# The last head of a four-layer gated transformer: gated outputs and normalising moved from VectorE to ScalarE and GpSimd

## The reference

```python
x = x + jnp.tanh(g_xattn[3]) * _L3_xattn_ref(_layernorm(x, axis=-1), ctx_4096, ctx_4096, pos_BxS2, mask_BxSxS2_ik0, L3_xattn_Wq, L3_xattn_Wk, L3_xattn_Wv, L3_xattn_Wo)
x = x + jnp.tanh(g_ffn[3]) * _L3_ffn_ref(_layernorm(x, axis=-1), L3_ffn_A, L3_ffn_B, L3_ffn_Wr)
```

## Time and profile before

| | before |
|---|---|
| median of 3 runs | 2186.48 us (2184.53 to 2188.93) |
| the profiled execution | 2186.74 us |
| its span | 2184.9 us |
| mean granted TensorE clock | 0.912 of full speed |
| last turn, first to last tile's `add_out` | 2003.22 to 2162.09 us in the span |

### The profile page before, as it was taken

How to read it: one execution, slowest core, us unless ns; L and a number is a source line. 1 busy time by engine, 2 the same in 40 slices (tenths; PEclk the granted TensorE clock), 3 DMA queues, 4 the chain that set the end, 5 groups by cost and what they waited for, 6 DMA issues and landing times. The chain is left out here.

```text
span 2184.9 us, 37129 instructions
## 1 busy us (share of the span) xinstructions
PE 1860.1 (85%) x14832; PEld 1034.9 (47%) x14832; DVE 1671.9 (77%) x2989; ACT 557.4 (26%) x1290; POOL 599.5 (27%) x717
## 2 busy tenths in 40 slices
PE   4388788887788888988855899999999999999876
PEld 3344455444554355533632355555555555555432
DVE  3379766798658966699644788888888888888875
ACT  3121223222342123222224122222222222222221
POOL 0220114102140023300224443434343434343210
PEclk7689978999899987999967999999999999999987
DMA  7436501473033720436013211111111111110100
GB/s 231 154 103 191 152 2 39 132 204 111 1 103 115 204 63 1 137 116 174 1 43 127 78 49 49 49 49 49 49 50 51 52 51 51 49 30 20 40 25 35
DMA packets 134266, 176.47 MB, mean 81 GB/s; under 512 B 46416, under 2 KB 73200, under 8 KB 133968
## 3 DMA queue, kind: packets, MB, share of 16 engines
q1 hardware_dynamic: 134096, 174.10, 26.5%
HBM read 131.98 MB, written 42.08 MB: 80 GB/s over the span
## 5 line engine op out<-in xcount | busy, mean ns | idle before, releaser
L1156 POOL TENSOR_TENSOR early_vare<-early_mv,w_eps 128x1 f32<-128x1 f32 x96 | 30.1, 313 | 779.0 <-DVE early_mv L1222 764.9
L379 PE MATMUL la_ps<-w_xTh,w_wqh 128*128 128x512 bf16 x512 | 198.4, 388 | 15.4 <-DVE la_rot L2271 10.3
L2210 POOL TENSOR_TENSOR la_q<-la_straight,la_rot 128x512 f32<-128x512 f32 x128 | 163.1, 1274 | 164.7 <-DVE la_rot L2271 164.7
L379 PE MATMUL la_ps<-w_woh,la_oTh 128*128 128x512 bf16 x512 | 199.2, 389 | 0.0
L380 PE MATMUL la_ps<-w_wol,la_oTh 128*128 128x512 bf16 x512 | 198.8, 388 | 0.0
L750 PE MATMUL early_ps<-early_products,w_heads 128*32 128x512 f32 x1024 | 146.0, 698 | 61.0 <-DVE early_products L1373 34.9
L381 PE MATMUL la_ps<-w_woh,la_oTl 128*128 128x512 bf16 x512 | 197.8, 386 | 0.0
L380 PE MATMUL la_ps<-w_xTl,w_wqh 128*128 128x512 bf16 x512 | 196.7, 384 | 0.0
L381 PE MATMUL la_ps<-w_xTh,w_wql 128*128 128x512 bf16 x512 | 196.6, 384 | 0.0
L2223 POOL TENSOR_TENSOR la_p<-la_s,la_rec 128x256 f32<-128x256 f32 x128 | 89.6, 700 | 322.4 <-DVE la_rec L2292 322.4
L2161 ACT ACTIVATE la_oTh<-la_ps 128x256 bf16<-128x256 f32 x256 | 84.2, 381 | 303.1 <-PE la_ps L2073 303.1
(11 more groups left out here) (345 smaller groups left out, 4535.2 us busy)
## 6 DMA issues: line engine op xcount, KB each, us to landing
early_vR<-scr_v SPq DMA_DIRECT2D x128, 257.0 KB, 5.2
early_wkv<-wkv SPq DMA_DIRECT2D x32, 512.0 KB, 4.6
la_v<-v SPq DMA_DIRECT2D x64, 256.0 KB, 3.9
k<-early_ctxt SPq DMA_DIRECT2D x32, 256.0 KB, 3.7
v<-early_ctxt SPq DMA_DIRECT2D x64, 128.0 KB, 3.1
scr_p<-early_weights SPq DMA_DIRECT2D x16, 512.0 KB, 3.1
early_pR<-scr_p SPq DMA_DIRECT2D x32, 256.0 KB, 3.4
w_raw_q<-in_Wq SPq DMA_DIRECT2D x8, 1024.0 KB, 6.9
```

Of the source, the lines that this page charges most:

```text
L379: pe.matmul(out, lh[c], rh[c], start=(first and c == 0), stop=False)
L2210: rope_sum.send(pool.tensor_tensor(dst, straight[:, slot, :], rot[:, slot, :], ALU.add))
```

## The change

The last turn alone changes, in units 1 to 15 and behind them.

- **Output of the attention.** `add_out` of tiles 0 to 15 goes from VectorE. ScalarE copies the bank times the gate into `gated` (`out_copy`, two buffers in `raw_q`, free by then), and GpSimd adds it to x (`add_x`). `statistics` waits for `x_added`.
- **Normalising.** `normalised` goes from VectorE to ScalarE as one activation with scale and bias; GpSimd computes the bias (minus the mean times the factor) with two more small operations in `rstd_of`. ScalarE does `normalised(i-2)` behind `exponentials` and `route_exp` of unit i; VectorE did it at the end of unit i-1.
- **Output of the experts.** `final` goes from VectorE: ScalarE copies the bank times the gate into `moved` (`move_copy`), GpSimd adds x (`final`), and SyncE's stores wait for `finished` in place of the drained bank.
- **Low half of the turned x.** `low_x` goes from the gap behind the subtraction of the softmax to behind the rotation, before `statistics`.
- TensorE's stream is the same. One more constant is set (`minus_one`, with `pads` counted to 4).

The diff, cut to its core and shifted left by 8 columns:

```diff
+minus, offset, minus_one = sb("minus", [P, 2]), sb("offset", [P, 2]), sb("minus_one", [P, 1])
+gated, moved = raw_q[:, 0:2, :], raw_q[:, 2:4, :]
...
+x_added, offset_ready, finished = signal("x_added", UNITS), signal("offset_ready", UNITS), signal("finished", UNITS)
...
     for t in range(UNITS):
-        banks.wait_drained(sp, KV - 1, "add", t)
+        finished.wait(sp, 0, t)
         stored[t % 2].send(sp.dma_start(io["out"][t * P:(t + 1) * P, :], xout[:, t % 2, :]))
...
+    def out_copy(t):
...
+        banks.wait_filled(act, KV - 1, "out", t // QUAD, t % QUAD, "last")
+        banks.drain(act.activation(gated[:, t % 2, :], banks.bank("out", t // QUAD, t % QUAD, "last"), ACT.Copy,
+                                   scale=w["gates"][:, 3:4]), "out", t // QUAD, t % QUAD, "last")
+
+    def normalised(t):
+        offset_ready.wait(act, 0, t)
...
+        xn_ready.send(act.activation(xn[:, t % 2, :], w["X"][:, t, :], ACT.Identity,
+                                     scale=rstd[:, t % 2:t % 2 + 1], bias=offset[:, t % 2:t % 2 + 1]))
...
+    def move_copy(t):
...
+        banks.wait_filled(act, KV - 1, "add", t)
+        banks.drain(act.activation(moved[:, t % 2, :], banks.bank("add", t), ACT.Copy,
+                                   scale=w["gates"][:, 7:8]), "add", t)
...
                 if not more and i >= 3:
                     route_exp(i - 3)
                 if not more and i >= 2:
+                    normalised(i - 2)
                     high_x(i - 2)
                 banks.wait_filled(act, turn, "turn", n, u, *L)
                 banks.drain(act.activation(pT[:, u % 2, :, :].rearrange("p h k -> p (h k)"),
                                            banks.bank("turn", n, u, *L)[:, 0:2 * P], ACT.Copy),
                             "turn", n, u, *L)
+                if not more and i >= 1:
+                    out_copy(i - 1)
                 if not more and i >= 4:
...
                         oTh[:, u % 2, :, :].rearrange("p (a b) t -> p a b t", b=2)[:, :, half, :],
                         banks.bank(name, n, u, *L)[:, 0:2 * P].rearrange("p (h t) -> p h t", h=2), ACT.Copy))
+                if not more and i >= 4:
+                    move_copy(i - 4)
                 if not more and i >= 2:
                     route_copy(i - 2)
...
+                    normalised(i - 2)
                     high_x(i - 2)
+                if i == UNITS:
+                    out_copy(UNITS - 1)
                 hsT_copy(i - 4)
+                move_copy(i - 4)
                 if i - 2 < UNITS:
                     route_copy(i - 2)
...
     def rstd_of(t):
         s = slice(t % 2, t % 2 + 1)
...
         pool.tensor_tensor(vare[:, s], mv[:, t % 2, 1:2], w["eps"][:, :], ALU.add).then_inc(pool_step, 1)
+        pool.tensor_tensor(minus[:, s], mv[:, t % 2, 0:1], minus_one[:, :], ALU.mult).then_inc(minus_step, 1)
         pool.wait_ge(pool_step, t + 1)
+        if t >= 2:
+            xn_ready.wait(pool, 0, t - 2)
         rstd_ready.send(pool.tensor_tensor(rstd[:, s], vare[:, s], w["power"][:, 0:1], ALU.pow))
+        pool.wait_ge(minus_step, t + 1)
+        rstd_ready.wait(pool, 0, t)
+        offset_ready.send(pool.tensor_tensor(offset[:, s], minus[:, s], rstd[:, s], ALU.mult))
+
+    def add_x(t):
+        banks.wait_drained(pool, KV - 1, "out", t // QUAD, t % QUAD, "last")
+        x_added.send(pool.tensor_tensor(w["X"][:, t, :], w["X"][:, t, :], gated[:, t % 2, :], ALU.add))
+
+    def final(t):
+        banks.wait_drained(pool, KV - 1, "add", t)
+        if t >= 2:
+            stored[t % 2].wait(pool, 0, t // 2 - 1)
+        finished.send(pool.tensor_tensor(xout[:, t % 2, :], w["X"][:, t, :], moved[:, t % 2, :], ALU.add))
...
                 if more or (n, u) != (QUAD - 1, QUAD - 1):
                     divide(turn, QUAD * n + u + 1, (u + 1) % 2)
+                if not more and at >= 1:
+                    if at == 1:
+                        pool.wait_ge(pads, 4)
+                    add_x(at - 1)
+                if not more and at >= 5:
+                    final(at - 5)
                 for i, place, which, step in projections(n, u, more):
                     add_rotation(turn, place, (len(FIRST) + i) % 2, rotated(which, step))
...
                 if not more and (n, u) != (0, 0):
                     rstd_of(QUAD * n + u - 1)
         if not more:
+            add_x(UNITS - 1)
             rstd_of(UNITS - 1)
+            for t in range(UNITS - 5, UNITS):
+                final(t)
...
         shifted_ready.send(dve.tensor_tensor(s[:, slot, :, :], s[:, slot, :, :],
                                              mx[:, slot, :].unsqueeze(2).to_broadcast([P, GROUP, SEQ]),
                                              ALU.subtract))
-        if meanwhile is not None:
-            low_x(meanwhile)
         exp_ready.wait(dve, turn, i)
         st.link(dve.tensor_reduce(tot[:, slot, :], s[:, slot, :, :], AX.X, ALU.add))
         rec_ready.send(dve.reciprocal(rec[:, slot, :], tot[:, slot, :]))
...
     def statistics(t):
-        banks.wait_drained(dve, KV - 1, "out", t // QUAD, t % QUAD, "last")
+        x_added.wait(dve, 0, t)
         fs.link(dve.bn_stats(stats[:, t % 2, :], w["X"][:, t, :]))
         stats_ready.send(dve.bn_aggr(mv[:, t % 2, :], stats[:, t % 2, :]))
-
-    def normalised(t):
-        dve.wait_ge(rstd_ready.sem, t + 1)
-        xn_ready.send(dve.tensor_scalar(xn[:, t % 2, :], w["X"][:, t, :], mv[:, t % 2, 0:1],
-                                        rstd[:, t % 2:t % 2 + 1], ALU.subtract, ALU.mult))
...
-    def final(t):
-        banks.wait_filled(dve, KV - 1, "add", t)
-        if t >= 2:
-            stored[t % 2].wait(dve, 0, t // 2 - 1)
-        banks.drain(dve.scalar_tensor_tensor(out=xout[:, t % 2, :], in0=banks.bank("add", t),
-                                             scalar=w["gates"][:, 7:8], in1=w["X"][:, t, :], op0=ALU.mult,
-                                             op1=ALU.add), "add", t)
...
                 if prev:
                     lows(*prev)
-                if not more and i >= 5:
-                    final(i - 5)
                 if more or (n, u) != (QUAD - 1, QUAD - 1):
                     softmax(turn, st, ("score", n, u, *L), (u + 1) % 2, QUAD * n + u + 1,
-                            (QUAD * n + u + 1) % (QUAD * QUAD), i - 2 if not more and i >= 2 else None)
-                else:
-                    low_x(i - 2)
+                            (QUAD * n + u + 1) % (QUAD * QUAD))
                 for p, place, _, step in projections(n, u, more):
                     rotate(turn, len(FIRST) + p, (len(FIRST) + p) % 2, place, step)
-                if prev:
+                if prev and (more or i == 0):
                     add_out(*prev)
                 if (n, u) == (0, 0) and not is_first(turn):
                     banks.wait_drained(dve, turn - 1, "out", QUAD - 1, QUAD - 1)
                 if not more:
+                    if i >= 2:
+                        low_x(i - 2)
                     if i >= 1:
                         statistics(i - 1)
                     if i >= 3:
                         choose(i - 3)
-                    if i >= 1:
-                        normalised(i - 1)
         if more:
             st.close()
         else:
             lows(turn, QUAD - 1, QUAD - 1, *L)
-            for i in range(UNITS, UNITS + 5):
-                if i - 3 < UNITS:
-                    logits(i - 3)
-                final(i - 5)
+            for i in range(UNITS, UNITS + 3):
+                logits(i - 3)
                 if i - 2 < UNITS:
                     low_x(i - 2)
                 if i == UNITS:
-                    add_out(turn, QUAD - 1, QUAD - 1, *L)
                     statistics(UNITS - 1)
-                if i - 3 < UNITS:
-                    choose(i - 3)
-                if i == UNITS:
-                    normalised(UNITS - 1)
+                choose(i - 3)
```

More of the change, by code:

```diff
@@ L1862, in last_attention @@
         hs_ready = signal("hs_ready", UNITS)
+        x_added, offset_ready, finished = signal("x_added", UNITS), signal("offset_ready", UNITS), signal("finished", UNITS)
+        minus_step = new_semaphore(nc, w, "la_minus_step")
         stored = [signal(f"stored{p}", UNITS // 2, 16) for p in range(2)]
@@ L2134, in high_x @@
                                             ACT.Copy))
+            def out_copy(t):
+                if t >= 2:
+                    x_added.wait(act, 0, t - 2)
+                banks.wait_filled(act, KV - 1, "out", t // QUAD, t % QUAD, "last")
[4 more added lines that the diff above has]
+                if t >= 2:
+                    banks.wait_filled(act, KV - 1, "xturn", t - 2)
+                xn_ready.send(act.activation(xn[:, t % 2, :], w["X"][:, t, :], ACT.Identity,
+                                             scale=rstd[:, t % 2:t % 2 + 1], bias=offset[:, t % 2:t % 2 + 1]))
+            def move_copy(t):
+                if t >= 2:
+                    finished.wait(act, 0, t - 2)
```

(10 more changed lines are left out.)

## The result

The changed kernel takes 2231.31 us (median of 4 runs, 2218.19 to 2238.51) against 2187.7 for the kernel before (4 runs): a ratio of 1.0195, with a 95% interval of 1.016 to 1.0229. It is slower, as forecast, but by 43.6 us and not by 22, and it lies outside the range of 2199 to 2219. The profiled execution took 2227.45, 40.7 more than that of before.

What follows compares the result with a forecast made beforehand. The prediction took a loop through all of x's path as the bound. Second stretch 17.3, first 0.4, tail 2.4 and sharing 1.9 made 22.0 us more, 2208.5 us against the median of 2186.48, range 2199 to 2219.

Steps and rivals of the forecast that it cites:

- the faster rivals: Last turn, cases below the forecast: VectorE relief pays, 2175 (0.05); only first stretch gains, 2192 (0.05); nothing much, 2187 (0.03).
- Steps 1, 3 and 4: Loop after the output projection lands: copy and addition, statistics at 2.04 us; normalising starts at 6.86, takes 0.80.
- step 2: Loop, statistics and choice of experts on VectorE: stay at 2.21 us, ending 4.25 after the output projection lands.
- Step 3: Loop, ScalarE: normalising waits behind the next unit's exponentials, which wait for VectorE; starts 6.86 us after the landing.
- the first rival: Relief of VectorE pays, normalising not held behind exponentials: second-stretch period 10.4, first 14.3 us less, total 2175; chance 0.05.
- Step 5, second stretch: Last turn's later seven periods, turning of x to the next output projection's landing: 5.70 us, ends 5.16 and 6.5.
- The tail: From the last output projection's landing to the end of the last `final`: 18.84 us, 2.4 more than before.
- Step 5, first stretch: Last turn's first eight periods, turning of x to the next landing: 3.48 us, TensorE's idle time staying near 2.2.
- The sharing term: GpSimd's rotation sum slowing VectorE's choice in six first-stretch units: 0.31 us each, 1.9 in all, ends 0 and 7.6.
- the fallen clock: Rival: clock falls in the first stretch too, 3.48 becoming 5.16 in six units; 10 us more, 2218.5; chance 0.10.
- the full hold: Rival: GpSimd's additions hold VectorE up in full; 5.7 us more, 2214; chance 0.07.

Runs made afterwards that it cites:

- e2: The changed kernel with ScalarE's normalising put ahead of the exponentials; ratio 1.0025 to the kernel before.
- e1: The changed kernel with GpSimd's order alone altered, rotation sums ahead of `add_x` and `final` behind `rstd_of`; ratio 1.013 to the kernel before.
- e3: The changed kernel with 10 or 18 unread matmuls a unit ahead of TensorE's wait for the normalised x; ratio 1.0066 to the kernel before.
- p_final_only: The kernel before with the experts' output alone moved (copy on ScalarE, addition on GpSimd); ratio 0.9948 to the kernel before.

## Why the prediction was wrong

- **The kernel's bound** was read rightly: the loop through x, not VectorE's load. TensorE's wait for `la_xn` and VectorE's for `add_x` are the long ones, and the faster rivals fall.
- **Steps 1, 3 and 4** hold to 0.1 us; step 2's 2.21 became 3.28 by the hold (below). Step 3, the one that decided the sign, is shown by e2: with normalising not held behind the exponentials, 36.3 of the turn's 41.7 extra us go, of which 13.6 are quicker work of TensorE that follows from it. The periods of the second stretch, 10.5, are the 10.4 that the first rival had for this case.
- **Step 5, second stretch:** 5.59 measured, 5.70 said. **The tail:** 2.7 measured, 2.4 said.
- **Step 5, first stretch, failed:** "so I take 3.48". The turning of x to the landing took 4.95 to 5.25 in five of the six units, and 5.08 in the first of all. With a sixth unit of 6.21 that is 12.6 us more than forecast. The forecast kept the clock of a unit whose idle time ahead was 2.11, and said that it would stay near 2.2; it was 2.98 in the plain units, because of the next point (1.91 in e1, where the hold is gone). e3 shows the cost, 12.1 us in that stretch with the clock at 1.00. The hold isn't the whole reason: the first unit lost its clock behind an idle time of 2.21 with no choice of experts yet, and one unit of e1 behind 1.91. What decided it in these two stays open.
- **The sharing term, "I take 0.31 each, 1.9 in all", failed by size:** 5.6 us in the units that it was for, by the two copies alone, and 8.3 over the turn. The row that I took it from began when only 0.45 us of a GpSimd division were left (2030.62 to 2031.07); an addition of 1.27 us that starts first holds for what is left of it, up to 0.81 more for `la_pick`. I had a whole addition for each as the upper end, 7.6. The four operations that I had named lost 0.06 us at most in the changed kernel (`la_sel`, 0.22 on the mean for 0.16); the copies, which I had left out, were held.
- **The Trainium skill on the hold** (SBUF — State Buffer, "Who interferes with whom"): by its rule the loser blocks. `la_sum`'s 1.17 and `la_comb`'s 1.19 agree with it. That section also counts copies among the operations that can take the shared ports; `la_pick`'s 0.98 agrees.
- **The rivals as alternatives.** I had the fallen clock at 10 us more and the full hold at 5.7 more, each by itself. They are not independent: the hold makes idle time, and the clock falls with it. In the profiled executions, repairing one alone saves 12.2 or 12.1 us in the first stretch, both 15.5. Added to the forecast, both give 2224. The profiled execution took 2227.45.

## What to carry to other kernels

In a loop that runs through several engines, moving a step to an idle engine lengthens the loop by the extra steps and by whatever stands ahead of the moved one in that engine's order. Of the four parts here, only the one that left the loop altogether, the experts' output, paid by itself; the order on the receiving engine decided most of the rest (e2). GpSimd additions that read SBUF belong where VectorE has no copy and no operation with two SBUF inputs. Delays that look separate should be priced together where one makes the idle time that brings down TensorE's clock.

## What the runs showed of the hardware that was not expected

- A hold passes on: with the copies replaced, the next operation with two SBUF inputs waited for GpSimd's addition in their place (1.17 us), and maxima over one SBUF input passed at 0.12 and 0.15.
- Matmuls whose result nothing reads can pay: 10 to 18 a unit took 25.0 us off the changed kernel's turn, and 5 a unit took 4.2 off p_final_only's.
- The kernel before varied more than its three runs said: 2175 to 2199 us in one series of 19. The time ahead of the last turn in the profiles varied by 15 us, with no edit there (1992.49 to 2007.65).
